# Axial attention on one core: q and k transposed by DMA instead of TensorE and ScalarE, scores in two pairs of PSUM banks

## The reference, cut to what matters

```
scale = 1.0 / np.sqrt(HEAD_DIM)
logits = jnp.einsum('bqhd,bkhd->bhqk', q, k) * scale
w = jax.nn.softmax(logits, axis=-1)
attn = jnp.einsum('bhqk,bkhd->bqhd', w, v)
attn = attn.reshape(b, n, N_HEADS * HEAD_DIM)
return attn @ Wout + bout
```

## Time and profile before

| | us |
|---|---|
| median of 3 runs | 1546.27 |
| lowest and highest run | 1543.81, 1550.5 |
| span of the profiled execution | 1552.5 |

### The profile page before, as it was taken

One profiled execution on the slowest core, in us unless ns is written; L12 is line 12 of the kernel. 1 busy time (PEld: TensorE's weight loads), 2 busy tenths in 40 slices (PEclk: granted clock), 3 DMA queues, 4 the chain that ended last, 5 costly groups with the idle time before them and its releaser, 6 DMA issues.

```text
span 1552.5 us, 21490 instructions
## 1 busy us (share of the span) xinstructions
PE 1348.3 (87%) x6917; PEld 940.6 (61%) x6925; DVE 1055.0 (68%) x2217; ACT 760.9 (49%) x1887; POOL 209.3 (13%) x221
## 2 busy tenths in 40 slices
PE   7788779968999667999998599976999999869998
PEld 4444446644444335677766489975888888744554
DVE  7999977887764697788787632226666666575564
ACT  5787723454875474655554212214666666422221
POOL 0123210010000001221111072111111111010000
PEclk9899979985986678999999789997999999968999
DMA  5222240000000200000004098845222121000100
GB/s 181 81 95 81 95 170 1 1 0 2 5 4 4 79 0 1 1 0 35 34 1 116 6 343 314 304 167 184 68 72 70 68 76 66 21 0 17 34 34 27
DMA packets 36418, 111.02 MB, mean 72 GB/s; under 512 B 4693, under 2 KB 15966, under 8 KB 30992
## 3 DMA queue, kind: packets, MB, share of 16 engines
q1 hardware_dynamic: 34464, 105.75, 19.3%
q0 software_dynamic: 1872, 4.22, 0.7%
HBM read 84.66 MB, written 26.21 MB: 71 GB/s over the span
## 4 chain that ended last, share of the span: by engine, by line
PE 66%; DVE 17%; issue 7%; ACT 5%; DMA 3%; POOL 1%; SPq 1%; DVEq 0%; ACTq 0%; POOLq 0%
PE psum L3064 6%; DVE roomA L753 5%; PE psum L2376 4%; PE psum L2715 4%; PE psum L1958 4%; PE psum L873 4%; PE psum L2663 4%; PE psum L2693 3%; PE psum L2000 3%; PE psum L2741 3%; PE psum L3074 3%; PE psum L2385 2%; PE psum L1338 2%; PE psum L1990 2%; PE psum L1370 2%
## 5 line engine op out<-in xcount | busy, mean ns | idle before, releaser
L2780 ACT ACTIVATE roomA<-psum,roomA 128x256 f32<-128x256 f32 x128 | 70.9, 559 | 92.7 <-DVE roomA L2845 92.4
L1516 DVE TENSOR_REDUCE roomB<-psum 128x2 f32<-128x512 f32 x128 | 83.9, 689 | 42.7 <-PE psum L1338 41.6
L2046 ACT ACTIVATE roomA<-psum,roomA 128x128 f32<-128x128 f32 (+1 forms) x128 | 53.2, 426 | 88.4 <-DVE roomA L2121 88.3
L3064 PE MATMUL psum<-roomA,roomB 128*128 128x512 f32 (+1 forms) x192 | 91.9, 623 | 0.3 <-ACT roomA L3171 0.3
L2515 DVE SCALAR_TENSOR_TENSOR roomA<-roomA,psum 128x512 f32<-128x512 f32 x23 | 15.8, 689 | 103.2 <-ACT roomA L2420 103.2
L1958 PE MATMUL psum<-own,roomB 128*128 128x512 f32 x160 | 75.1, 594 | 3.4 <-DVE roomA L2113 2.1
L1921 POOL TENSOR_TENSOR roomA<-roomA 128x512 f32<-128x512 f32 x40 | 50.9, 1273 | 176.9 <-DVE roomA L2114 176.9
L2715 PE MATMUL psum<-roomA 128*128 128x256 f32 x256 | 68.3, 389 | 6.0 <-DVE roomA L2857 4.4
L753 DVE TENSOR_TENSOR_SCAN roomA<-roomA 128x1024 f32<-128x1024 f32 x32 | 73.1, 2284 | 0.0
L2693 PE MATMUL psum<-roomA 128*128 128x256 f32 x256 | 65.6, 379 | 1.7 <-ACT roomA L2780 1.7
L873 PE MATMUL psum<-own,roomB 128*128 128x512 f32 x144 | 66.7, 608 | 0.0
(11 more groups left out here) (509 smaller groups left out, 3400.7 us busy)
## 6 DMA issues: line engine op xcount, KB each, us to landing
roomB<-m_w_dram SPq DMA_DIRECT2D x12, 1536.0 KB, 9.1
roomA<-m_w_dram SPq DMA_DIRECT2D x11, 1536.0 KB, 9.0
a_kv_ready<-roomB SPq DMA_DIRECT2D x32, 512.0 KB, 3.1
roomA<-a_kv_ready SPq DMA_DIRECT2D x8, 1024.0 KB, 4.8
roomA<-a_kv_ready SPq DMA_DIRECT2D x16, 512.0 KB, 4.1
roomB<-a_w_dram SPq DMA_DIRECT2D x4, 1280.0 KB, 6.3
roomB<-f_w_dram SPq DMA_DIRECT2D x8, 624.0 KB, 3.9
m_rows<-roomA SPq DMA_DIRECT2D x1, 2978.5 KB, 15.3
```

The costliest lines, as they stand in the source:

```text
L1516: dve.tensor_reduce(maxneg[:, hp // 8, :, m, hp % 8], g.bank(m).rearrange("p (q k) -> p q k", k=S), AX.X, ALU.max, negate=True).then_inc(s ...
L3064: ins = pe.matmul(g.bank(bank, rows=m), w[:, kt, at:at + m], xg[:, n % 2, kt, half * HALF:(half + 1) * HALF], start=(kt == 0), stop=(kt == ...
```

## The change

The T entries go. SP issues 32 DMA transposes (`turn`) in their place, each of 128 tokens x 8 pairs x 128 columns of bf16: four for each half batch, one semaphore for each half. The order on SP is: keys of batch 0 when the constants and keys stand, queries of batch 0 when the first two query tiles stand, then, when all query tiles stand and batch 0 is turned, batch 1; after that the maxima's stores and loads (`shift`), and behind each from the second on the four transposes of a later half, once the scores that read the buffer are through.

Banks 6 and 7 are free of the ring. Scores take the pairs 2, 3 and 6, 7 in turn throughout, and the transposed maxima take a turn in the same order (`users`, `pair_of`, `pair_free`). The results of the batches are transposed and multiplied in banks 0 and 1 at steps 64, 65, 66 and 81, when the maxima are over. The list `ring` is replaced by `M_STEP` and `AT_STEP`.

```diff
+    AT_BANK, OUT_BANK = (0, 1, 0, 0), (1, 0, 1, 1)
...
-    ring = [(-1, "T", 0, k) for k in range(4)] + [(k, "T", 0, 4 + k) for k in range(4)]
-    ring += [(16 * t - 10 + 2 * k, "T", t, k) for t in range(1, B) for k in range(8)]
-    ring += [(16 * t + 8 * hf + 9, "M", t, hf) for t in range(B) for hf in range(2)]
-    ring += [(max(16 * t + LAG + 20, 53 + 2 * t), "A", t, 0) for t in range(B)]
...
+    AT_STEP = [64, 65, 66, 16 * (B - 1) + LAG + 20]
+    M_STEP = {16 * t + 8 * hf + 9: 2 * t + hf for t in range(B) for hf in range(2)}
...
+    users = []
+    for step in range(STEPS):
+        if 0 <= step - LAG < B * HP:
+            users.append(("scores", step - LAG))
+        if step in M_STEP:
+            users.append(("maxima", M_STEP[step]))
+
+    def pair_of(*user):
+        return (2, 6)[users.index(user) % 2]
+
+    def pair_free(pe, *user):
+        j = users.index(user)
+        if j >= 2:
+            kind, n = users[j - 2]
+            pe.wait_ge(s["a1_exp" if kind == "scores" else "a1_mt"], n + 1)
+
+    def turned(t, hf):
+        return s[f"a1_tr{hf}"], 64 * t + 64
...
     def sync(sp):
+        def turn(which, t, hf):
+            dst = (trQ, trK)[which][t % 2]
+            for r in range(2):
+                src = aug[which][:, 2 * t + r, 16 * hf:16 * hf + 16, :].rearrange("p h c -> p (h c)")
+                sp.dma_start_transpose(dst[:, 8 * hf:8 * hf + 8, r * P:(r + 1) * P], src).then_inc(turned(t, hf)[0], 16)
+
+        def shift(t, hf):
+            sp.wait_ge(s["a1_mt"], 2 * t + hf + 1)
+            sp.dma_start(shifts[t, hf], partsT[:, hf, :]).then_inc(s["a1_stored"], 16)
+            sp.wait_ge(s["a1_stored"], 32 * t + 16 * hf + 16)
+            for m in range(2):
+                row = PARTS * HD + SLOT * m
+                sp.dma_start(trQ[t % 2][row:row + 3, 8 * hf:8 * hf + 8, :],
+                             shifts[t, hf].rearrange("(c m h) q -> c m h q", c=3, m=2)[:, m]).then_inc(s[f"a1_rows{hf}"], 16)
+
+        sp.wait_ge(s["a1_ones"], 3)
+        for sem in ("a1_aug", "a1_dup1", "a1_dup2"):
+            sp.wait_ge(s[sem], NT)
+        for hf in range(2):
+            turn(1, 0, hf)
+        for sem in ("a1_aug", "a1_dup1", "a1_dup2"):
+            sp.wait_ge(s[sem], NT + 2)
+        for hf in range(2):
+            turn(0, 0, hf)
+        for sem in ("a1_aug", "a1_dup1", "a1_dup2"):
+            sp.wait_ge(s[sem], 2 * NT)
+        for hf in range(2):
+            sp.wait_ge(*turned(0, hf))
+        for hf in range(2):
+            turn(1, 1, hf)
+            turn(0, 1, hf)
+        shift(0, 0)
+        for k in range(1, 2 * B):
+            shift(k // 2, k % 2)
+            t, hf = 2 + (k - 1) // 2, (k - 1) % 2
+            if t < B:
+                sp.wait_ge(s["a1_tsc"], HP * (t - 2) + 8 * hf + 8)
+                turn(1, t, hf)
+                turn(0, t, hf)
...
         def for_maxima(step, m):
             t, hp = step // HP, step % HP
             if hp % 8 == 0 and m == 0:
-                pe.wait_ge(s["a1_tr"], count_to(at_ring[("T", t, 4 * (hp // 8) + 3)]))
+                pe.wait_ge(*turned(t, hp // 8))
...
+        def turn_sums(t):
+            if t < 2:
+                pe.wait_ge(s["a1_max_read"], 2 * B * HP)
+            elif t < B - 1:
+                pe.wait_ge(s["a1_at"], t - 1)
             else:
+                pe.wait_ge(s["layer_done"], base + B - 2)
+            pe.wait_ge(s["a1_attn"], 4 * t + 4)
...
-            if n == SINGLE:
-                pe.wait_ge(s["a1_max_read"], 2 * B * HP)
-            elif n > SINGLE:
-                pe.wait_ge(s["a1_exp"], n - 1)
-            elif n:
-                pe.wait_ge(s["a1_exp"], n)
+            pair_free(pe, "scores", n)
...
+        pe.wait_ge(s["a1_proj_read"], 2 * NT)
+        for step in range(STEPS):
             e = step - LAG
-            if 0 <= e <= SINGLE:
+            if 0 <= e < B * HP:
                 scores(e)
-            elif SINGLE < e < B * HP and (e - SINGLE) % 2 == 1:
-                scores(e)
-                if e + 1 < B * HP:
-                    scores(e + 1)
...
-            while n < len(ring) and ring[n][0] == step:
-                entry(n)
-                n += 1
+            if step in M_STEP:
+                turn_maxima(M_STEP[step])
+            if step in AT_STEP:
+                turn_sums(AT_STEP.index(step))
```

More of the change, by code:

```diff
@@ L1300, in tensor @@
         pe.wait_ge(s["a1_v"], NT)
[L1301 to L1320, removed]
-            else:
[L1322 to L1328, removed]
@@ new lines, in turn_maxima @@
+        def turn_maxima(k):
+            t, hf = k // 2, k % 2
+            pair_free(pe, "maxima", k)
+            pe.wait_ge(s["a1_max"], k + 1)
+            for qt in range(2):
+                src = parts[:, t % 2, hf, qt].rearrange("p c h -> p (c h)")
+                ins = pe.transpose(g.bank(pair_of("maxima", k), rows=48).bitcast(BF16)[:, qt * P:(qt + 1) * P], src, g.identb)
+            ins.then_inc(s["a1_mt_psum"], 1)
+        def turn_sums(t):
[3 more added lines that the diff above has]
+                pe.wait_ge(s["a1_at"], t - 1)
+            else:
+                pe.wait_ge(s["layer_done"], base + B - 2)
+            pe.wait_ge(s["a1_attn"], 4 * t + 4)
+            for kt in range(KD):
+                for r in range(2):
+                    ins = pe.transpose(g.bank(AT_BANK[t])[:, (2 * kt + r) * P:(2 * kt + r + 1) * P],
+                                       attn[:, 2 * t + r, kt * P:(kt + 1) * P], g.ident)
+            ins.then_inc(s["a1_at_psum"], 1)
@@ L1354, in scores @@
                     rows = slice(SLOT * m, SLOT * m + ROWS)
-                    ins = pe.matmul(g.bank(score_bank(n) + m)[:, kt * S:(kt + 1) * S], trK[t % 2][rows, hp, kt * P:(kt + 1) * P],
+                    ins = pe.matmul(g.bank(pair_of("scores", n) + m)[:, kt * S:(kt + 1) * S], trK[t % 2][rows, hp, kt * P:(kt + 1) * P],
                                     trQ[t % 2][rows, hp, :], start=True, stop=True)
@@ L1382, in project_out @@
         def project_out(t, r):
[L1383 to L1386 removed]
+            pe.wait_ge(s["a1_at"], (2, 3, 3, 4)[t])
             if t >= 2:
[L1388 removed]
+                pe.wait_ge(s["layer_done"], base + t - 1 + t // 3)
             i = 2 * t + r
             for kt in range(KD):
[L1391 removed]
+                ins = pe.matmul(g.bank(OUT_BANK[t])[:, r * D:(r + 1) * D], g.XT[:, kt, i * P:(i + 1) * P], w_out[:, kt, :],
                                 start=(kt == 0), stop=(kt == KD - 1))
@@ L1423, in tensor @@
                     project_out(t, r)
-        assert n == len(ring)
     def scalar(act):
@@ L1472, in scalar @@
                 act.copy(ot[:, q % 2, :], g.bank(4 + q % 2)).then_inc(s["a1_ot"], 1)
-            while n < len(ring) and ring[n][0] == step:
-                copies(n)
-                n += 1
+            if step in M_STEP:
+                maxima_in(M_STEP[step])
+            if step in AT_STEP:
+                sums_in(AT_STEP.index(step))
     def gpsimd(pool):
@@ L1559, in vector @@
                 g.f1_norm["root"](dve, 0, 6)
-                dve.wait_ge(s["a1_tr"], 8 * B)
+                for hf in range(2):
+                    dve.wait_ge(*turned(B - 1, hf))
                 g.f1_norm["apply"](dve, 0, 3)
```

67 lines of the change are left out of this document (14 added, 53 removed).

## The result

The changed kernel takes 1555.51 us (median of 16 runs, 1547.85 to 1563.33) against 1547.53 for the kernel before (16 runs, 1540.86 to 1558.21). The range held it, the sign was wrong.

The account below looks back on a forecast made before the run. VectorE's reductions plus their waits for the maxima matmul, and the granted clock, were taken as the bounds. Head -3.4, long stretch -6.9 and tail +1 sum to -9.3 us: 1546.3 to 1537 us, range 1525 to 1564.

Parts of the forecast that it names:

- the base: Whole kernel: a difference worked out within the profiled execution of 1552.5 us is subtracted from the median, 1546.3 us.
- What bounds a step: Long stretch: a step lasts VectorE's 76 us of reductions plus 36 us of bubbles; only a shorter bubble shortens it.
- Head, -3.4: Before the first reduction: with DMA transposes at 2.0 us of queue each, it starts at 349.5 instead of 352.89, -3.4 us.
- Maxima only, 0: The 13 steps computing only maxima: pace taken as it was, 0 us.
- Full clock, 1.89 a step: Long stretch at full clock: the 0.70 us bubble falls to about 0.15, so eight steps take 15.15 instead of 16.25 us.
- Half clock, 2.53 a step: Long stretch at half clock: shorter TensorE waits for exp and VectorE save about 0.6 of 10.8 us per four steps.
- The share of half rate, 35%: Long stretch: TensorE's busy share hardly changes, so half-rate time goes from 30% to 35%; 105.8 us, -6.9.
- Tail, +1: After the long stretch: sums of batches 0 and 1 now transposed there, adding copies and transposes, +1 us (0 to +2).
- A: Long stretch: the clock eats the gain, 60% at half rate, total 1545 us; entirely at half rate 1560; chance 0.20.
- B: SP's queue: transposes above 2.1 us each delay the maxima's store and load; 1548 to 1576 us; chances 0.10 and 0.12.
- C: DMA transposes: each 128-column block a transfer after the last, 14.4 us a DMA, total 1816 us; chance 0.04.
- D: Long stretch: full clock throughout, since ending the exp waits keeps TensorE dense; total 1528 us; chance 0.12.

Follow-up runs that it names:

- the kernel with fill at the splits: Changed kernel plus unread transposes at VectorE's splits: sixteen in the split's step, eight ahead of the next step's first maxima; 1533.28 us, ratio 0.9914.
- the run with sixteen in the split's step: Changed kernel plus only sixteen unread transposes between the two maxima of each step where VectorE splits the maxima; 1531.59 us, ratio 0.9868.
- the second run: Changed kernel plus eight unread transposes in every second step with scores and in each of the 13 maxima-only steps; 1551.47 us, ratio 1.0023.

## Why the prediction was wrong, point by point

**The sum against the outcome.** Forecast were 1537 us, measured 1555.5. In the two profiles the layer took 2.3 us more instead of 9.3 less: 11.6 of the 18.5 us are the terms below. The other 7 come from the base. "So I work out a difference within this execution and subtract it from the median": with every term as measured this would still give 1546.3 + 2.3 = 1548.6, because the profiled execution had a lower clock (0.915) than the runs mostly have (0.921). Read against an execution with a low clock, a loss of clock comes out too small. That this execution lost its clock in this layer is not shown; only one execution of before was profiled.

**What bounds a step (right).** "A step lasts as long as VectorE's reductions plus their bubbles." With the clock held, eight steps of 1.92 follow from the same sum, and the two bubbles behind the value matmuls stayed at 0.6, as said.

**Head, -3.4 (right).** Measured -3.4, by the mechanism named: VectorE's memset sets the start. The transpose's queue time was taken as 2.0 us and is 1.36, which changes nothing there.
The Trainium skill (DMA: Bandwidth & Descriptors, "Latency and other measured facts") gives 261 GB/s, hence some 1.0 us for 256 KB, an estimate; measured are 256 KB / 1.36 us = 193 GB/s, and the measurement decides.

**Maxima only, 0 (wrong by -2.3).** The step took the pace of before as it was. But eight T entries stood among these steps, 1.03 us each of a TensorE at half clock; without them it is busy 14.5 of 20.3 us, no longer 20.9 of 23.7, and the part is 2.3 us shorter.

**Full clock, 1.89 a step (nearly right).** Measured 1.92, in the kernel with fill at the splits. The bubble of 0.70 fell to 0.25 or 0.42 rather than 0.15.

**Half clock, 2.53 a step (mis-sized).** Measured, eight steps with a split, from VectorE's timeline of after:

```profile
431.63 2.08 DVE L1525 TENSOR_REDUCE roomB<-psum 128x2 f32<-128x512 f32 x3
435.38 0.69 DVE L1525 TENSOR_REDUCE roomB<-psum 128x2 f32<-128x512 f32 x1 [1.67 <-PE psum L1370]
...
446.11 2.08 DVE L1525 TENSOR_REDUCE roomB<-psum 128x2 f32<-128x512 f32 x3 [1.67 <-PE psum L1370]
...
453.86 2.08 DVE L1525 TENSOR_REDUCE roomB<-psum 128x2 f32<-128x512 f32 x3
```

(453.86 - 431.63) / 8 = 2.78. The four steps I worked from the earlier trace rows held no split, and I booked 0.15 a step for the end of the waits for exp. They ended, and this gave nothing: four steps without a split took 446.11 - 435.38 = 10.7 us, as before. At half clock the value matmuls (1.89 us) set the step, seen in VectorE's bubbles of 1.67.

**The share of half rate, 35% (the step of the sum that failed).** "TensorE's busy share at full clock hardly changes (the 0.54 goes, and the period shortens by the same)." It fell from 91% to 73%. Four T entries went in eight steps (in the trace of before at 404.74, 408.30, 412.48 and 416.05), not two: 4 x 0.6 = 2.4 us of TensorE, while the eight steps shortened by 16.25 - 15.36 = 0.9 (at full clock, with fill at the splits). That alone makes (0.91 x 16.25 - 2.4) / 15.36 = 81%. I had counted the two that made a bubble, and let the two that filled one go for nothing; one of these, at 416.05, was TensorE's cover at the split. The rest goes with scores and maxima whose records now overlap in time (two starts at 395.90 and 395.91, for one), with the idle time in one piece behind them: the waits for VectorE rose from 4.5 to 18.9 us. With the measured share and the forecast's paces the stretch is 113.6, with the measured paces too 51 / (0.4/1.92 + 0.6/2.78) = 120 against 121.9 measured. So of the 15 us between the forecast (106.9, first scores to last reduction) and the outcome about 8 are the share and 7 the paces.

**Tail, +1 (wrong by 1).** Measured -0.1. The clock in it was 0.89, before 0.82, and may have hidden the cost.

**The rivals.** A came true, even in its number: 60% at half rate. Its time of 1545 was too low by the half-clock pace and by the base. That the clock is the cause is shown by the fill, which only adds work: ratio 1.0044 without it, 0.9868 with it, and mean clock 0.908 and 0.929. Which property of the lost work held the clock is not shown. B would have decided at 2.1 us of queue; at 1.36 it fell, and TensorE waited for a transpose only up to 347.50. (The maxima's load did hold TensorE up once, 1.15 us, in the run with sixteen in the split's step.) C needed eight landings one after the other, 14.4 us; the DMA landed in 3.4. D (1528) is nearly what the kernel with the clock held does.
The Trainium skill (VectorE: DVE Perf Modes, "The three transpose paths") has 1309 ns per block by DMA; here eight blocks took 1.36 us of the queue and 3.4 to landing.

**What stays open.** Without the sixteen the half-rate share is 60% in after, 74% in the run without late DMAs and 78% in the run with eight transposes behind the split. Why these differ was not found, nor why the clock of one kernel differs from run to run (0.910 to 0.929 in before); whether it depends on how the stalls lie against the clock was not tried. How few transposes in the split's step would do was not tried either, nor eight there against eight a step later.

## What to carry to other kernels

Before work is taken off TensorE, look at where its stalls stand and what stands beside them: the work may be what holds the clock, and the price of losing it (here some 20 us in one layer) can exceed that of the work. Read the busy share in the granted-clock windows again after the change, not the busy total. If the clock drops behind a known stall, add transposes whose result nobody reads around it and measure each place by itself: sixteen ahead of the split's second maxima gave 0.9868, eight in the longest wait just behind it 1.0087. Compare runs at equal granted clock too, when each run has one: that showed here that the change was sound and the clock was not. And before a profile serves as the base of a sum, compare its clock with those of the runs.

## What the runs showed of the hardware that was not expected

- The granted clock fell behind waits of TensorE of only 1.36 us, with the engine 73% busy around them, and once behind 0.67 us with 91% busy (before, at 434). It stayed at 1.00 with 87% busy and waits up to 0.6 us (378 to 434, sixteen and eight at the splits), and with 82% busy and waits of 1.00 (399 to 453, the sixteen alone).
- With TensorE 93% busy for 25.5 us (48-row maxima and 128-row transposes) it stayed at 0.50 (the second run), and with 96% busy for 40 us of the steps with scores too (371 to 411, eight behind the split). The busy count of the profile does not foretell the clock.
- A DMA transpose of 128 x 1024 bf16 inside SBUF costs SP's queue 1.36 us and lands in 3.3. With the clock held, the long stretch took 99.4 us with sixteen of them beside the compute and 99.1 without.
- Taking DMAs away did not make the kernel faster (1.0075 against 1.0044; the intervals overlap), and the clock of the stretch was lower (0.63 against 0.70).
- The time of one unchanged kernel moved over 20 us between 84 runs, with its mean granted clock: 1540.4 us at 0.929, 1556 to 1561 at 0.910 to 0.911.
